# Attention in two graph layers on one core: value products in bursts of a whole query tile, VectorE and ScalarE steps at other units

## What is computed

```
h  = relu(layernorm(x))                      # x: after layer 0 ("y" in the kernel)
xp = L_norm @ h;  z = xp @ Wc + bc           # L_norm 512 x 512, for all batches
x1 = relu(layernorm(z) * g1 + be1) + h
q, k, v = x1 @ Wq, x1 @ Wk, x1 @ Wv          # 4 heads of 32
s  = where(adj > 0, q k^T / sqrt(32), -1e9)
o  = softmax(s) v @ Wo + bo
x2 = layernorm(x1 + o) * g2 + be2
out = x + layernorm(x2 + mlp(x2)) * g3 + be3
```

## Time and profile before

| | |
|---|---|
| median of 3 runs | 1019.43 us (1019.34 to 1019.48) |
| profiled execution | 1022.98 us, span 1021.2 us |
| busy over the span | PE 932.9 us, DVE 630.3, ACT 519.3, POOL 325.5 |
| mean granted clock of TensorE | 0.955 |
| attention stage | about 500 to 915 us of the span |
| last stage (MLP) | about 915 us to the end |

### The profile page before, as it was taken

How to read it: one execution, slowest core, us unless ns; L and a number is a source line. 1 busy time by engine, 2 the same in 40 slices (tenths; PEclk the granted TensorE clock), 3 DMA queues, 4 the chain that set the end, 5 groups by cost and what they waited for, 6 DMA issues and landing times. The chain is left out here.

```text
span 1021.2 us, 19958 instructions
## 1 busy us (share of the span) xinstructions
PE 932.9 (91%) x7030; PEld 749.2 (73%) x7030; DVE 630.3 (62%) x2077; ACT 519.3 (51%) x1127; POOL 325.5 (32%) x405
## 2 busy tenths in 40 slices
PE   5998899999999999999699999999999999979982
PEld 4556799999999999988477777777777777656651
DVE  3752333333333333524588888988888888764998
ACT  2222322222222232210688888888888887765540
POOL 0001111111111111203234555544455543226775
PEclk8887999999999999989799999999999999998996
DMA  3000000000000000004354444444444444500111
GB/s 90 1 1 10 11 1 21 10 10 10 10 10 10 10 10 10 12 1 121 85 135 114 120 114 122 116 115 117 111 125 112 117 125 125 125 2 11 52 44 60
DMA packets 47218, 61.54 MB, mean 60 GB/s; under 512 B 4377, under 2 KB 22050, under 8 KB 47138
## 3 DMA queue, kind: packets, MB, share of 16 engines
q1 hardware_dynamic: 47138, 60.51, 22.9%
HBM read 39.53 MB, written 20.97 MB: 59 GB/s over the span
## 5 line engine op out<-in xcount | busy, mean ns | idle before, releaser
L1540 ACT ACTIVATE prob<-prob,low 128x512 f32<-128x512 f32 x256 | 184.0, 719 | 51.5 <-DVE low L1590 49.5
L1590 DVE CUSTOM_DVE_ANT_0 prob<-bank,mask 128x512 f32<-128x512 f32 x256 | 171.3, 683 | 28.3 <-PE bank L1419 26.7
L1432 PE MATMUL bank<-ident,prob 128*128 128x128 f32 x1024 | 161.9, 281 | 12.5 <-ACT probT L1529 12.3
L1432 PEld LDWEIGHTS bank<-ident,prob 128*128 128x128 f32 x1024 | 113.9, 141 | 58.3 <-issue 31.2
L1419 PE MATMUL bank<-k_stack,q_stack 128*128 128x512 f32 x256 | 123.8, 485 | 9.9 <-DVE low L1590 5.0
L1529 ACT ACTIVATE probT<-bank 128x512 f32<-128x512 f32 x176 | 102.5, 583 | 2.8 <-PE bank L1432 1.1
L1065 DVE TENSOR_TENSOR T_lo<-bank,T_hi 128x512 fp32r<-128x512 f32 x48 | 33.0, 688 | 112.0 <-ACT T_hi L903 112.0
L601 POOL TENSOR_SCALAR var_eps<-mv 128x4 f32<-128x4 f32 x16 | 3.6, 226 | 297.3 <-DVE mv L1018 297.3
L903 ACT ACTIVATE T_hi<-bank 128x512 fp32r<-128x512 f32 x48 | 28.4, 592 | 134.7 <-PE bank L813 91.7
L909 ACT ACTIVATE Sq<-bank,trace_inv 128x512 fp32r<-128x512 f32 x64 | 43.9, 686 | 92.3 <-PE bank L736 92.3
L1452 PE MATMUL bank<-probT,v 128*32 128x128 f32 x2048 | 82.3, 279 | 3.1 <-ACT probT L1529 1.1
(11 more groups left out here) (232 smaller groups left out, 1943.9 us busy)
## 6 DMA issues: line engine op xcount, KB each, us to landing
k_stack<-bounce_q SPq DMA_DIRECT2D x64, 256.0 KB, 5.0
q_stack<-bounce_k SPq DMA_DIRECT2D x64, 256.0 KB, 7.5
bounce_q<-k_parts SPq DMA_DIRECT2D x16, 512.0 KB, 2.8
bounce_k<-q_parts SPq DMA_DIRECT2D x16, 512.0 KB, 3.2
x_in<-in_x_dram SPq DMA_DIRECT2D x16, 256.0 KB, 2.7
out_dram<-result SPq DMA_DIRECT2D x16, 256.0 KB, 2.2
A<-in_adj_dram SPq DMA_DIRECT2D x4, 256.0 KB, 3.2
W1s<-in_L_gnn_W_dram SPq DMA_DIRECT2D x1, 128.0 KB, 2.2
```

The costliest lines, as they stand in the source:

```text
L1432: last = pe.transpose(psum[2 + u % 2][:, mt * P:(mt + 1) * P], prob[u % RING][:, mt * P:(mt + 1) * P], ident[:, :])
L1540: act.activation(prob[u % RING][:, :], prob[u % RING][:, :], ACT.Exp, bias=low[:, u % TURNED:u % TURNED + 1], scale=-1.0, accum_out=row_su ...
L1590: dve.tensor_tensor_reduce(prob[u % RING][:, :], psum[u % 2][:, :], mask[:, u // HEADS, :], 1.0, 3e38, ALU.add, ALU.min, low[:, u % TURNED ...
```

## The change

The table moves steps, and `h_scales` moves ahead of the z2 steps in GpSimd's loop.

```
-AT_Y_MOMENTS, AT_H = 9, (11, 12, 13, 15)
+AT_Y_MOMENTS, AT_H = 0, (10, 11, 12, 13)
 AT_RINV, AT_SPREAD, AT_SPREAD_OUT, AT_O, AT_PROJ, AT_Z2 = 0, 3, 4, 8, 11, 12
-AT_Z2_MOMENTS, AT_Z2_STD = 3, 5
+AT_Z2_MOMENTS, AT_Z2_STD = 4, 8
 TURN_LAG = 3
 VALUES_LAG = 7
-VALUES_STEP = 2
-DVE_COPIES = (0, 7, 11, 13, 15)
+VALUES_STEP = 4
+DVE_COPIES = (3, 6, 10, 12, 13)
...
                     if within(r, 1, BATCH - 2):
                         split_h(r + 1, 1 - s)
+                    if within(r, 0, BATCH - 3):
+                        h_scales(pool, one, r + 2, s)
                     e = r - 3
...
-                    if within(r, 0, BATCH - 3):
-                        h_scales(pool, one, r + 2, s)
                     if enters:
                         add_bo(r, s)
```

## The result

| | before | changed |
|---|---|---|
| median of 5 runs each | 1019.48 us (1019.34 to 1021.21) | 1056.86 us (1050.99 to 1057.97) |
| ratio | | 1.0363, 95% interval 1.0328 to 1.0398 |
| profiled execution, span | 1022.98, 1021.2 us | 1050.99, 1049.2 us |
| transposes of x1 (L321), first to last | 466.9 to 865.0, 398.1 us | 463.2 to 894.2, 431.0 us |

The change makes the kernel 3.6% slower: the sign is as forecast, the time inside the range. The profiled execution is the fastest of the five. Of its 28.0 us over the profile of before, the stretch between the first and the last transposes of x1 has 32.9; what comes ahead of it is 3.7 shorter and what follows 1.2 shorter.

A forecast was written before the change was run, and what follows sets the result against it. One round's loop through the engines bounds it, TensorE only in d and e, VectorE and ScalarE in a, b, c. Pieces of 27.6 plus waits 0.3, 0.57, 0.3 make 28.8 us (+2.45); +31 us overall, 1050.5, range 1033 to 1070.

The forecast's parts named there:

- b: VectorE from mask 13 to mask 2 of the next round: 6.70 us grows to 8.42, plus a 0.3 wait.
- c: Mask 2 to the spread transposes, through ScalarE: 2.17 us grows to 2.65 by a copy priced at 0.48.
- a: Output projections to VectorE's mask of unit 13: 3.05 us, unchanged.
- d: Spread transposes, key product and value burst of unit 3, TensorE the bound: 1.99 us grows to 2.42.
- e: TensorE from unit 4 to the next projections: 12.44 us falls to 11.1, before new waits of 0.57 and 0.3.
- The turn of unit 7: TensorE waits there for ScalarE's copy of unit 2: 3.46 us after the query product, a new wait of 0.57.
- The product with W_c: At unit 10 it loses a burst's cover against ScalarE's copy of the convolution: a wait estimated at 0.3 us.
- A pause of about 0.3: Single waits on TensorE's path near the burst of unit 7, about 0.3 us, counted as gone.
- The clock: Rival: TensorE's granted clock falls in attention, losing about 1.7 us in each of 13 rounds, 1072 us; chance 0.12.
- Faster: Rival: VectorE's steps from mask 13 leave the path, only the 20 us burst saving counts, 1000 us; chance 0.04.
- it does not matter: Rival: savings in d and e cancel additions in b and c, so no change; chance 0.03.
- The loop alone: Rival: the loop lengthens but none of the new waits come, +15 us, 1034 us; chance 0.11.

The follow-up runs named there:

- e4: The kernel before with the moments of y moved to unit 0 and nothing else: ratio 1.0133.
- e2: The changed kernel with the moments of y back at unit 9, and the h steps and GpSimd's order as before: ratio 1.0132.
- e3: The changed kernel with the copies shared as before (VectorE has units 0, 7, 11, 13, 15): ratio 1.0212.
- e8: The kernel before with long bursts, VectorE copies at 2, 3, 6, 7, 15, moments of y at 7, h at 10 to 13, z2 at 3 and 6: ratio 1.0134.
- e7: The kernel before, short bursts kept, VectorE copies at units 0, 4, 6, 7, 15, moments of y at 6, h at 9 to 12: ratio 0.9982.
- e1: The kernel before with longer bursts alone (VALUES_STEP 4 for 2): ratio 1.0086.
- e6: e1 with the z2 steps of the change, at units 4 and 8: ratio 1.0015.
- e9: The changed kernel with five idle identity products on TensorE ahead of the scores of unit 2: ratio 1.0308, median 1051.29 us.
- e10: The changed kernel unaltered, run a third time, beside e9 on the same chip: 1057.0 us.
- e5: The changed kernel unaltered, run once more as one traced execution: 1052.49 us.
- e12: The kernel before, short bursts, convolution, W_c product and z steps a unit earlier, with moments of y, h and copies moved: ratio 1.0294.

## Why the prediction was right, and where it was off

- **Sign and mechanism.** Right. The loop changes engine, VectorE and ScalarE are the bound in b and c of the changed kernel, and work put there is paid, in full where no slack is left: e4 (b +0.96) and e2 (b -1.31) show it for the moments of y, e3 for the copies (c -0.49, b -0.32). Of the signs that it named, the score of unit 3 waits (1.34 us); that of unit 4 does not (724.03, 0.39 behind its turn).
- **a, b, c, d.** 3.11, 8.43, 2.65, 2.43 us against 3.05, 8.42 and 0.3 of wait, 2.65, 2.42. The wait in b came (0.24 at the copy of unit 13, behind a burst that waits 0.47), but the step from residual to mask 2 took 0.76 us, not the 0.98 of the earlier trace rows, and gave it back; that was luck, since the forecast has no term for it. The timelines show what goes with it: in before the residual takes 1.06 us and lies 0.52 beside GpSimd's copy of the inverses (678.27 above), in the changed kernel 0.84 and 0.29, in e8 0.71 and none of that copy. That the one slows the other is not tested by itself. GpSimd's timeline of the changed kernel:

```profile
721.77 0.61 POOL L1373 COPY rinv<-sums_inv 128x512 f32<-128x512 f32 x1 [1.69 <-DVE sums_inv L1606]
```

- **b before.** The prediction names the pause between mask 1 and the residual, but not its cause: it is the wait for GpSimd's z_norm, as shown under e7. So before the change VectorE was not alone the bound of b; after it, it was.
- **e.** 12.03 against 11.97, and its terms came nearly as put, one of them by luck. The turn of unit 7 stands 732.13 - 728.66 = 3.47 us behind the query product (3.46 forecast), of which 0.30 shows as a wait. The product with W_c starts 738.28 - 737.79 - 0.32 = 0.17 late, and from it to the next transposes it takes 0.12 longer (0.3 forecast in all). "A pause of about 0.3" near the burst of unit 7 is gone: from the turn there to the burst it was 689.62 - 687.85 = 1.77 us before and is 733.62 - 732.13 = 1.49. But the prediction gave no reason why it should go, and of the moved z2 steps it says "I cost both at nothing". It is these that take it away: with the bursts alone the same way is 1.93 us (e1), with the z2 steps 1.48 (e6). Beside long bursts they are worth 0.44 us a loop; that term was missed. TensorE's timeline of before, the burst of unit 7 in the loop of the earlier trace rows:

```profile
689.62 0.65 PE L1452 MATMUL bank<-probT,v 128*32 128x128 f32 x16
```

- **The parts are no plain sum.** e1 +0.63, e4 +0.96, copies +0.77 (28.65 less e3's 27.88) and z2 steps -0.44 make +1.92; together they made 2.28. The difference, 0.36, is that of e2 and e4 (1.31 - 0.96): the slack of b, 0.12 ahead of the residual and 0.23 behind it (0.23 in all in the forecast), can be used up once, and the moments of y alone used it.
- **How many loops.** 11 loops of 29.01 - 26.42 are 28.5 us (27 forecast); the whole stretch is 32.9 longer, so the other ways paid 4.4 (4.2 forecast).
- **The rivals.** *The clock* holds by the sign that the prediction gave for it, a fall within attention, and is a term that the forecast lacks; its price was not that of the rival: the clock fell six or seven times, at 0.45 to 0.9 us of loop time each and 2.7 for a long fall, not 1.7 in each of 13 rounds. The Trainium skill's page TensorE: Matmul & The Clock Gate (Why this matters for your kernels) has the rule that idle gaps bring the lower clock; the trace agrees that they can, with the 3.40 us at 0.50, and e9 that filling one keeps it away. *Faster* and *it does not matter* fall with e1: TensorE's saving alone ends 0.9% slower. The Trainium skill's page TensorEngine Tiling (Array Packing) (Key Properties) says that a change of tiling mode drains the array; what that costs did not set the time here. *The loop alone* falls too: the new waits were there.
- **The median.** It is 6.4 us above the forecast. The attention stretch of e10, an execution near the median, is 36.5 us longer than before's, 5.5 over the 31 forecast; without falls (e9) it is 29.5 longer. So the falls are the larger part of the miss. The remaining 0.9 lies outside that stretch or in the spread between executions; no run says which.

## What to carry to other kernels

Where several engines are nearly full, follow one loop through them and ask of each moved step on which engine's piece it lands: the same 1.34 us of VectorE cost nothing where TensorE was the bound and 1 to 1.3 us per round where VectorE was. A saving on the busiest engine pays only where that engine is the one waited for; here an estimated 20 us less of TensorE's work, alone, ended 0.9% slower. Follow every input of a step: the residual also waits for GpSimd, and e7 gained no more than that left. Test parts apart and by taking them out again, since slack that one part uses up is missing for the next.

## What was not expected of the hardware

The same waits of TensorE in every round (1.34, 0.26 and 1.00 us in the loop shown) brought the granted clock from 1.00 to 0.50 (2.4 to 1.2 GHz) in some rounds only. In the first profile that is every second round, at 520.1, 578.1, 636.2, 694.2, 752.2 and 810.2 us, 58 us apart, for 3.4 us each. In e5 and e10 the first three falls come in rounds that follow each other (546.2, 577.0 and 607.7 us in e5), the middle one for 6.8 us, and the rest 58 us apart. About 1.28 us of idle products a round kept the clock at 1.00 (e9). A burst of 32 in one tiling takes 1.01 us to the next group, as the 0.107 us per four matmuls had it. And steps of VectorE took longer beside certain steps of GpSimd: z_std 1.93 us, not 1.12, beside x1_bo (e12), the residual 0.71 to 1.06 us by how long it lay beside the copy of the inverses.
